# Scores of four heads at a time, read where the projections lie

## What is computed

```python
xn = _layernorm(x)
qkv = einsum('bsd,ed->bse', xn, w_qkv) + b_qkv          # 16 heads of 32 for q, k, v
scores = einsum('bhqd,bhkd->bhqk', q, k) / sqrt(32) + causal
attn = softmax(scores, axis=-1)
out = einsum('bhqk,bhkd->bhqd', attn, v)                # then @ w_out.T + b_out
hdn = silu((xn @ gate_w.T) * gate_s) * ((xn @ up_w.T) * up_s)
result = x + attention + (hdn @ down_w.T) * down_s
```

## Time and profile before

| | us |
|---|---|
| median of 3 runs (lowest, highest) | 1981.75 (1980.51, 1983.86) |
| the profiled execution | 1987.12 |
| its span, first to last instruction | 1984.8 |
| PE busy | 1878.5 (95%) |
| DVE busy | 1695.7 (85%) |
| ACT busy | 1352.8 (68%) |
| POOL busy | 1137.4 (57%) |

### The profile page before, as it was taken

One profiled execution on the slowest core, in us unless ns is written; L12 is line 12 of the kernel. 1 busy time (PEld: TensorE's weight loads), 2 busy tenths in 40 slices (PEclk: granted clock), 3 DMA queues, 4 the chain that ended last, 5 costly groups with the idle time before them and its releaser, 6 DMA issues.

```text
span 1984.8 us, 43852 instructions
## 1 busy us (share of the span) xinstructions
PE 1878.5 (95%) x14978; PEld 1217.9 (61%) x14978; DVE 1695.7 (85%) x5012; ACT 1352.8 (68%) x3784; POOL 1137.4 (57%) x1624
## 2 busy tenths in 40 slices
PE   6689999999999999999999999999899999999996
PEld 4456576666656666566666756666566666756663
DVE  5778989988898898989889898888888888898885
ACT  4666676866767677676767767676576766767673
POOL 4565655657476475655657475464554656465352
PEclk9799999999999999999999999999999999999998
DMA  8987978789697887978788797786967778786784
GB/s 215 222 152 140 183 137 182 150 153 179 130 192 131 167 172 139 185 135 175 154 145 185 136 186 126 152 163 119 178 128 160 155 137 175 133 182 125 128 155 92
DMA packets 818837, 310.24 MB, mean 156 GB/s; under 512 B 756464, under 2 KB 789232, under 8 KB 818608
## 3 DMA queue, kind: packets, MB, share of 16 engines
q1 hardware_dynamic: 800928, 249.44, 69.6%
q0 software_dynamic: 17680, 57.95, 10.3%
HBM read 55.59 MB, written 16.78 MB: 36 GB/s over the span
## 4 chain that ended last, share of the span: by engine, by line
PE 48%; DVE 31%; DMA 5%; SPq 5%; ACT 5%; issue 3%; POOL 1%; DVEq 0%; ACTq 0%; POOLq 0%
PE bank L287 48%; DVE phl L587 8%; DVE bank L577 6%; DMA pt<-phl 5%; SPq L927 4%; ACT phl L479 3%; DVE fh L599 3%; DVE small L568 2%; DVE ft L595 2%; DVE res L611 2%; DVE xhl L723 2%; DVE xs L559 1%; ACT bank L487 1%; DVE small L549 1%; SPq L934 1%
## 5 line engine op out<-in xcount | busy, mean ns | idle before, releaser
L479 ACT ACTIVATE phl<-bank,small 128x512 f16<-128x512 f32 (+3 forms) x1024 | 500.0, 531 | 285.9 <-DVE small L568 221.9
L487 ACT ACTIVATE bank<-bank,small 128x512 f32<-128x512 f32 (+3 forms) x1024 | 513.6, 502 | 184.3 <-DVE small L577 176.8
L587 DVE SCALAR_TENSOR_TENSOR phl<-bank,small,phl 128x512 f16<-128x512 f32 (+3 forms) x1024 | 525.1, 544 | 72.1 <-ACT phl L479 67.9
L577 DVE CUSTOM_DVE_ANT_0 bank<-bank,mask 128x512 f32<-128x512 f32 (+3 forms) x1024 | 486.0, 505 | 104.1 <-PE bank L287 103.6
L788 POOL TENSOR_SCALAR ht<-fh 128x256 f16<-128x256 f32 x352 | 148.1, 421 | 438.1 <-DVE fh L599 437.9
L287 PE MATMUL bank<-xnT,wg 128*128 128x256 f16 x2816 | 368.3, 274 | 9.0 <-DVE fh L599 7.5
L287 PE MATMUL bank<-xnT,wu 128*128 128x256 f16 x2816 | 366.3, 273 | 0.0
L287 PE MATMUL bank<-xnT,wqkv 128*128 128x512 f16 x1536 | 352.1, 379 | 2.1 <-ACT q L452 2.1
L287 PE MATMUL bank<-wd,ht 128*128 128x512 f16 x1408 | 320.6, 384 | 4.6 <-ACT wd L430 3.9
L287 PEld LDWEIGHTS bank<-xnT,wg 128*128 128x128 f16 x2816 | 263.3, 98 | 73.4 <-DVE fh L599 8.0
L287 PEld LDWEIGHTS bank<-xnT,wu 128*128 128x128 f16 x2816 | 276.3, 98 | 32.7
(11 more groups left out here) (108 smaller groups left out, 2089.8 us busy)
## 6 DMA issues: line engine op xcount, KB each, us to landing
stk<-qkp SPq DMA_DIRECT2D x768, 64.0 KB, 2.2
res<-in_x_dram POOLq DMA_DIRECT2D x64, 256.0 KB, 4.7
xin<-in_x_dram POOLq DMA_DIRECT2D x60, 256.0 KB, 4.6
out_dram<-res POOLq DMA_DIRECT2D x60, 256.0 KB, 4.0
pt<-phl SPq DMA_TRANSPOSE x512, 4.3
xin<-in_gate_dram POOLq DMA_DIRECT2D x11, 256.0 KB, 4.1
xin<-in_up_dram POOLq DMA_DIRECT2D x11, 256.0 KB, 3.5
xin<-in_down_dram POOLq DMA_DIRECT2D x11, 256.0 KB, 3.9
```

The source lines that it names most:

```text
L479: i = eng.activation(phl[qt][:, j % 2, 0], pb[:, off:off + W], ACT.Copy, scale=st_r[:, c:c + 1])
L487: i = eng.activation(pb[:, off:off + W], pb[:, off:off + W], ACT.Exp, bias=st_m[:, c:c + 1], scale=-1.0, accum_out=st_s[:, c:c + 1])
L577: i = eng.tensor_tensor_reduce(out=bk[:, off:off + W], in0=bk[:, off:off + W], in1=mask[:, 512 - W:512], scale=-(32.0 ** -0.5) / (QS * QS) ...
L587: i = eng.scalar_tensor_tensor(phl[qt][:, j % 2, 1], pb[:, off:off + W], st_r[:, c:c + 1], phl[qt][:, j % 2, 0], ALU.mult, ALU.subtract)
```

## The change

It takes away `stk` and its DMAs. `scores(G, part)` now makes the scores of all four heads of a group together, in three parts: query tile 3; tiles 2 and 0; tile 1. Each part runs the three products one after the other, accumulating in PSUM, and each product as four matmuls in row tiles of 32 rows (`tile_position=(32 * j, 0)`), one per head, from `qkp` as it is. Head j always writes bank j. The parts stand in slots 3 and 7, and, for the first part of the next group, in slot 9. A part waits until `exponent` of all units before it is done (`a_exp`).

The exponentials no longer stay in PSUM: `exponent` writes them to four SBUF buffers `p32`, from which `high` and `low` read. `segs` is ordered by query tile, and `MAX_AT`, `REC_AT`, `EXP_AT` and `OUT_AT` say in which slots the steps of each unit stand. `phl` is double, one for each pair of heads. q and k are made one group ahead instead of two. `dtmp` shares the buffer of `xs32`, and the order of the weight chunks and of a few `gate_up` is changed.

```diff
 def segs(u):
-    p, k = divmod(u, 5)
-    if k < 2:
-        return [(2 * p + k, 3, 0)]
-    if k < 4:
-        return [(2 * p + k - 2, 2, 0), (2 * p + k - 2, 0, 384)]
-    return [(2 * p, 1, 0), (2 * p + 1, 1, 256)]
+    if u < 4:
+        return [(u, 3, 0)]
+    if u < 8:
+        return [(u - 4, 2, 0), (u - 4, 0, 384)]
+    return [(2 * u - 16, 1, 0), (2 * u - 15, 1, 256)]
...
-    stk = [sb(f"stk{i}", [96, 4, 2, 512], F16) for i in range(2)]
+    p32 = [sb(f"p32_{i}", [128, 512], F32) for i in range(4)]
...
+    MAX_AT = {0: (0, 1), 1: (2, 3), 4: (4, 5), 5: (6, 7), 8: (9,)}
+    REC_AT = {1: 0, 2: 2, 5: 4, 6: 6, 9: 8}
+    EXP_AT = {0: (0, 1), 1: (2, 3), 4: (4, 5), 5: (6, 7), 8: (8, 9)}
+    OUT_AT = {2: (0, 1), 3: (2, 3), 6: (4, 5), 7: (6, 7), 9: (8, 9)}
...
-    qk_at = {U * G + (1 if G % 4 == 3 and c == 0 else QK_K[c]): (G + 2, c) for G in range(NGRP - 2) for c in range(2)}
+    qk_at = {U * G + (1 if G % 4 == 3 and c == 0 else QK_K[c]): (G + 1, c) for G in range(NGRP - 1) for c in range(2)}
...
-        def scores(n):
-            G, u = divmod(n, U)
-            st, bk = stk[G % 2], bank[n % NSB]
-            w.wait_ge(d_stk[2 * (G % 2) + u // 5], 96 * (G // 2 + 1))
-            w.wait_ge(v_lo, n - NSB + 1)
-            for j, qt, off in segs(u):
+        def scores(G, part):
+            kp = qkp[G % 2]
+            w.wait_ge(p_ql, 2 * G + 2)
+            w.wait_ge(a_exp, U * G + 4 * part)
+            for qt, off in (((3, 0),), ((2, 0), (0, 384)), ((1, 0),))[part]:
                 W = 128 * (qt + 1)
-                i = mm(bk[:, off:off + W], st[:, j, 0, 128 * qt:128 * qt + 128], st[:, j, 1, 0:W], True, True)
+                for k, (qp, kp_) in enumerate(((1, 2), (1, 3), (0, 2))):
+                    for j in range(4):
+                        c = off if part < 2 else 256 * (j % 2)
+                        i = mm(bank[j][:, c:c + W], kp[32 * j:32 * j + 32, qp, 128 * qt:128 * qt + 128],
+                               kp[32 * j:32 * j + 32, kp_, 0:W], k == 0, k == 2, tile_position=(32 * j, 0))
...
-        qk(1, 0)
-        qk(1, 1)
         for f in range(F_FIRST):
             gate_up(f)
+        scores(0, 0)
         for n in range(LAST):
-            if n < NU:
-                scores(n)
+            G, k = divmod(n, U)
+            if n < NU and k in (3, 7):
+                scores(G, k // 3)
+            if n < NU - 1 and k == 9:
+                scores(G + 1, 0)
...
         def exponent(n):
...
-                i = eng.activation(pb[:, off:off + W], pb[:, off:off + W], ACT.Exp, bias=st_m[:, c:c + 1], scale=-1.0,
+                i = eng.activation(p32[n % 4][:, off:off + W], bank[j][:, a:a + W], ACT.Exp, bias=st_m[:, c:c + 1], scale=-1.0,
...
         def low(n):
...
-                i = eng.scalar_tensor_tensor(phl[qt][:, j % 2, 1], pb[:, off:off + W], st_r[:, c:c + 1], phl[qt][:, j % 2, 0],
+                i = eng.scalar_tensor_tensor(hl[:, j % 2, 1], p32[n % 4][:, off:off + W], st_r[:, c:c + 1], hl[:, j % 2, 0],
```

More of the change, by code:

```diff
@@ L28 @@
 U = 10
-NSB = 4
 NHT = 14
@@ L123, in fast_path @@
     d_small = [sem(f"d_small{i}") for i in range(5)]
-    d_w = [sem(f"d_w{i}") for i in range(15)]
+    d_w = [sem(f"d_w{i}") for i in range(16)]
     d_x0 = [sem(f"d_x0{i}") for i in range(4)]
@@ L140, in fast_path @@
         G, k = divmod(n, U)
-        for where in (2, 4, 5, 7, 8, 9) if G == 0 else F_WIN[G % 4]:
+        for where in (1, 2, 4, 5, 7, 8, 9) if G == 0 else F_WIN[1] if G == 2 else F_WIN[G % 4]:
             if k == where and f < NF:
@@ L262, in fast_path @@
         last = lambda i: max([m for m in range(n) if slot_of[m] == i], default=-1)
-        free = [i for i in range(len(stage)) if stage[i][1] > w_slot[n] and (n >= 12 or i < 12)]
+        free = [i for i in range(len(stage)) if stage[i][1] > w_slot[n] + (chunks[n][0] == "split") and (n >= 12 or i < 12)]
         slot_of.append(min(free, key=lambda i: (last(i), i)))
@@ L268, in fast_path @@
     stage = [buf for buf, n in stage]
-    w_load = [max([w_slot[n] - 4, 0] + [w_slot[before[n]] + 1] * (before[n] >= 0)) for n in range(NCH)]
+    done = [w_slot[n] + (chunks[n][0] == "split") for n in range(NCH)]
+    w_load = [max([w_slot[n] - 4, 0] + [done[before[n]] + 1] * (before[n] >= 0)) for n in range(NCH)]
     on_act = [sum(c[0] != "pool" for c in chunks[:n + 1]) for n in range(NCH)]
@@ L330, in av @@
             for qt in range(4):
-                w.wait_ge(d_pt[qt], 16 * (2 * G + 2))
+                for p in range(2):
+                    w.wait_ge(d_pt[qt][p], 16 * (G + 1))
             w.wait_ge(v_vl, 4 * b + 2 * (g // 2) + 2)
@@ L495, in scalar_program @@
             weight(t)
-        for n in range(4, 7):
+        for n in range(4, 6):
             weight(n)
         v_high(0, 0, 0)
-        weight(7)
         drain_qk(0, 0)
-        for n in range(8, 11):
-            weight(n)
-        drain_qk(0, 1)
-        weight(11)
-        v_high(0, 0, 1)
-        for n in range(12, W_FIRST):
-            weight(n)
-        drain_qk(1, 0)
-        drain_qk(1, 1)
+        weight(6)
+        drain_qk(0, 1)
+        weight(8)
+        weight(9)
+        v_high(0, 0, 1)
+        for n in range(10, W_FIRST):
+            weight(n)
         for f in range(F_FIRST):
@@ L520, in scalar_program @@
                 drain_av(av_at[n - 1])
-            if 2 <= n <= NU + 1:
-                high(n - 2)
             if n < NU:
-                exponent(n)
+                for u in OUT_AT.get(n % U, ()):
+                    high(n - n % U + u)
+                for u in EXP_AT.get(n % U, ()):
+                    exponent(n - n % U + u)
             if n - 1 in check_at:
@@ L691, in vector_program @@
         first_low(3)
-        for n in range(2, 7):
+        for n in range(2, 6):
             weight_low(n)
         v_low(0, 0, 0)
-        for n in range(7, W_FIRST):
+        for n in range(6, W_FIRST):
             weight_low(n)
@@ L708, in vector_program @@
                 hidden(f)
-            if 2 <= n <= NU + 1:
-                low(n - 2)
+            if n < NU:
+                for u in OUT_AT.get(k, ()):
+                    low(n0 + u)
+                if k == 7:
+                    maximum(n0 + 8)
             if n - 1 in v_at:
@@ L762, in split_qk @@
             i = 2 * G + c + 1
-            for p in range(2):
-                w.wait_ge(d_stk[2 * (G % 2) + p], 96 * (G // 2))
+            w.wait_ge(s_s, 3 * (G - 1))
             w.wait_ge(a_q32, i)
@@ L848, in gpsimd_program @@
         eng.tensor_scalar(cis[:, :], cis[:, :], 0.5 * HS / (XS * XS), 1.0, op0=ALU.mult, op1=ALU.mult).then_inc(p_set, 1)
-        for n in range(10):
-            weight(n)
+        weight(7)
         split_qk(0, 0)
         split_qk(0, 1)
-        for n in range(10, W_FIRST):
+        for n in range(8, W_FIRST):
             weight(n)
-        split_qk(1, 0)
-        split_qk(1, 1)
         w.wait_ge(d_small[3], 16)
```

132 lines of the change are left out of this document (56 added, 76 removed).

## The result

The changed kernel takes 2320.1 us (median, 2319.1 to 2320.4), the kernel before, run beside it, 1982.1 us: a ratio of 1.170, 95% interval 1.168 to 1.172. That is 338 us slower, where 56 us were forecast. The profiled execution has a span of 2318.2 us, 333.4 us more than before's 1984.8.

The account below looks back on a forecast made before the run. PE was taken to bound the kernel before, DVE after; 64 us more from `low` and DVE's waits, less 8 us at the start, gave +56 us on 1981.75, so 2038 us, range 1965 to 2120 us.

Parts of the forecast that it names:

- What bounds the kernel, and DVE as the deciding engine: Whole kernel: PE sets the pace before; after, DVE's added work exceeds its 3.1 us of room a group.
- `low` at 0.20 us more: DVE's `low`, now with two SBUF inputs, collides with POOL: 0.20 us each, 3.2 us a group; bounds 0.11 and 0.29.
- a random meeting with POOL at 0.22 us: Alternative estimate for `low` on DVE, meeting POOL's steps at random: 0.22 us each, making the sum 20 us higher.
- DVE's waits at 0.9 us a group: DVE's remaining idleness, taken as half of one group's 1.78 us before: 0.9 us a group, 3.6 us a batch.
- The hand-over as a rival: Four score banks given back together starve PE before a group's first part: 1.5 us a group, 96 us, 2070 us; chance 0.12.
- Row tiles even: PE's scores: four row tiles run abreast, 2.22 us a group with switches against 2.2 us before, counted as zero.
- The start, 8 us: Kernel start: first scores at about 28 us instead of 36.48, since q and k of group 1 move away; 8 us gained.
- The stack at nothing: Dropping the stack's 768 DMAs and their issues on SP: worth nothing in the middle of the run.
- PE's clock: PE's own list of work: no term for a change of its clock was included.
- The faster case, 0.17: DVE's room suffices if a `low` costs under 0.14 us more; PE sets the pace, 1931 to 1952 us; chance 0.17.
- The 43 us: Most that 14 middle batches could gain if each falls from 119.5 us to PE's 116.4.

Follow-up runs that it names:

- Experiment 2: Kernel before, with `low` reading its first input from a fixed SBUF tile instead of its PSUM bank; order and banks unchanged: 2110.9 us, 1.065.
- experiment 4: Changed kernel, POOL's main steps made zero fills that read nothing, maxima and exponents of units 8 and 9 moved to slot 7, maxima ahead of `low`: 1976.7 us, 0.997.
- experiment 3: Changed kernel, maxima of units 8 and 9 moved to the start of slot 7 ahead of `hidden` and `low`, their exponents into slot 7: 2149.1 us, 1.084.

## Why the prediction was right in sign and wrong in size

- **What bounds the kernel, and DVE as the deciding engine:** right. Experiment 2 shows the forecast mechanism at work: DVE at 91% and 129 us more in the old order.
- **`low` at 0.20 us more:** the mechanism was right, the term too small. Measured 0.27 us in the changed kernel (815 against 544 ns), 0.23 in the old order, within the bounds of 0.11 and 0.29. It gives 4.3 us a group instead of 3.2, and DVE's busy time rose by 269 us instead of 205. That 0.20 came this near is partly luck. L568 and L559, from which it and the upper bound were taken, have one tensor input (lines 559 and 568 of the kernel before); only L723 has two, and its mean said 0.11. Nor would the mean of L568 have done better than its median: 372 ns and 370. The forecast's other working, a random meeting with POOL at 0.22 us, is as near to the 0.23 of the old order.
- **DVE's waits at 0.9 us a group:** this is the step that failed. They are 4.9 us a group, above even the upper bound of 1.78, and DVE's idleness is 213 of the 277 us of the miss. The number was half of group B's idle time in the kernel *before*. It was too small already where only `low` was lengthened: 1.9 us a group in experiment 2, under the hand-over bank by bank. The other 3 us came with the hand-over of four banks, whose chain runs through DVE and ACT and back to PE: PE waits 5.0 us a group for the banks, and DVE's longest waits are now for PE's down products (85.9 us) and ACT's exponents (84.4 us). An idleness measured under one hand-over could not be carried over to another.
- **The hand-over as a rival:** its place, the two `gate_up` of cover and the eight `low` ahead of the maxima were all named, and the profile shows them. Two mistakes lie in its treatment. It was priced at 1.5 us a group with unlengthened `low`, where PE waits 5.0 us (321.3 / 64). And it stood as a rival with 0.12, as if it excluded the forecast. The two are not alternatives. From the 1976.7 us of experiment 4 the lock alone adds 172 us, the hand-over alone 98, and both together 343: they add, and 73 us come on top. The range ended at 2120 us because it held the hand-over at 96 us and only some of DVE's term.
- **Row tiles even:** right at full clock. The parts take 0.77 us (384 + 128), 0.44 (256) and 0.75 (512), 1.96 us a group against the 2.22 us of the sum. The 3.07 times in the Trainium skill, TensorE: Matmul & The Clock Gate, section on measured speedup in Part 3, would have made it an estimated 2.7 us; the trace does not bear it out for three products of four tiles in a row.
- **The start, 8 us:** measured 7.4 at the first score. What of it reaches the end is not shown by itself; experiment 4 ends 5.5 us below the kernel before. **The stack at nothing:** nothing in the runs speaks against it, but no run tests it alone.
- **PE's clock:** the forecast took PE's list as fixed. Behind long holes it isn't: behind the one of 9.9 us the clock was 0.68, and PE's busy time grew from 1878.5 to 1953.2 us, 75 us over the run.
- **The faster case, 0.17:** it hung on the lock costing under 0.14 us. Experiment 4 shows that even without the lock on `low` and with a relieved hand-over the time is only 0.3% lower. The 43 us that were thought to lie in PE's waits did not come: PE still waits 62.4 us for the banks there, where it waited 33.5 us before.

No version tried is faster than the kernel before by more than those 0.3%, and that one leaves POOL's reading steps out.

## What to carry to other kernels

Moving an operand of a DVE step from PSUM to SBUF can turn on a lock with POOL for every instance; count the SBUF inputs of each DVE step before and after. Price the lock as a range and not from one neighbour: here the neighbours said 0.11 to 0.29 us, it was 0.23 us in one order and 0.27 in another, and only a run such as experiment 2 settled it. Where a change replaces the way in which buffers are handed over, work out the new chain from end to end, with the lengthened steps in it, against the work that covers it, and add what sticks out to the rest of the sum: two costs on the same chain do not exclude each other, and together they can cost more than their sum (343 us here, against 172 and 98). If several buffers must come free together, put the last reader's work ahead of everything that merely has room, as the maxima in experiment 3 (171 us for two maxima and their exponents, placed earlier).

## What the runs showed of the hardware

- A DVE step with two SBUF inputs can lose to several POOL steps in a row: the `low` of 3.29 us at 664.86 was recorded 0.49 us before the next POOL compute step started, and ended 0.42 us after the second of them. The Trainium skill, SBUF — State Buffer, section on who interferes with whom, says of DVE's two-port modes that whoever issues first gets the shared pair for the whole instruction. For this step with two SBUF inputs the trace agrees in the pair of the earlier trace rows; in the case at 664.86 the order of the records does not show it, and why is open.
- POOL steps that only write leave such a DVE step alone: 548 ns with POOL busy for 710 us, against 544 ns from PSUM.
- Some DVE steps with one tensor input, in SBUF, are lengthened beside POOL too. The step of L568 before (L577 in the changed kernel, TENSOR_SCALAR on 4 columns) falls from 325 to 209 ns on the mean when POOL's main steps only write, that of L559 (L568 there) from 757 to 549. The RECIPROCAL beside it (L575), of the same shape and also from SBUF to SBUF, never takes more than 180 ns in the changed kernel. So counting the SBUF inputs does not find every step that collides.

```profile
L577 DVE TENSOR_SCALAR small<-small x320: 169/182/1297, 33.4 to 2290.0; 128x4 f32<-128x4 f32 x160
```

- The lock works both ways. POOL's two steps on the hidden values, L799 and L801 (L788 and L790 before), went from 421 to 542 ns and from 673 to 758 on the mean.
